# A selective-scan phase in which two gate blocks take their Silu after the scan, by an exponential and a reciprocal, and VectorE makes the first input product

## The reference, cut to what matters

```python
x_and_res = x @ in_proj_w.T + in_proj_b
x_b, res = jnp.split(x_and_res, [D_INNER], axis=-1)
...
x_b = jax.nn.silu(jnp.transpose(xc, (0, 2, 1)))
...
delta = jax.nn.softplus(delta @ dt_proj_w.T + dt_proj_b)
a = -jnp.exp(A_log)
y = _selective_scan(x_b, delta, a, b, c)   # h = exp(delta a) h + delta b x_b ; y = h c
y = y + x_b * D_param
y = y * jax.nn.silu(res)
return y @ out_proj_w.T + out_proj_b
```

## Time and profile before

| | us |
|---|---|
| median of 3 runs | 728.68 (724.33 to 729.57) |
| profiled execution | 728.93 |
| its span, first to last instruction | 727.2 |
| mean granted clock of TensorE, share of full | 0.962 |
| busy: PE, DVE, ACT, POOL | 667.5, 471.7, 367.1, 223.1 |

### The profile page before, as it was taken

How to read it: one execution, slowest core, us unless ns; L and a number is a source line. 1 busy time by engine, 2 the same in 40 slices (tenths; PEclk the granted TensorE clock), 3 DMA queues, 4 the chain that set the end, 5 groups by cost and what they waited for, 6 DMA issues and landing times. The chain is left out here.

```text
span 727.2 us, 11254 instructions
## 1 busy us (share of the span) xinstructions
PE 667.5 (92%) x4226; PEld 466.1 (64%) x4226; DVE 471.7 (65%) x809; ACT 367.1 (50%) x677; POOL 223.1 (31%) x181
## 2 busy tenths in 40 slices
PE   3989999999994999998989999899899989999998
PEld 1445555553353656565556788787777667889897
DVE  5123433448737998999989337576777658676554
ACT  1222111215476998998988333432456337447442
POOL 2000000000008999998976000032543002222000
PEclk9999999999996999999999999999989879999999
DMA  8999999738121232222220000000100012110000
GB/s 317 371 379 401 420 421 420 314 114 258 35 87 59 87 116 88 104 100 88 107 82 16 1 1 15 1 0 17 32 2 3 1 59 73 45 58 2 29 1 30
DMA packets 31069, 86.45 MB, mean 119 GB/s; under 512 B 7900, under 2 KB 19576, under 8 KB 28840
## 3 DMA queue, kind: packets, MB, share of 16 engines
q1 hardware_dynamic: 30456, 85.28, 32.2%
q10 hardware_dynamic: 560, 0.46, 0.3%
HBM read 83.50 MB, written 1.11 MB: 116 GB/s over the span
## 5 line engine op out<-in xcount | busy, mean ns | idle before, releaser
L683 POOL TENSOR_TENSOR dbu<-du,bs 128x1024 f32<-128x1024 f32 x64 | 150.8, 2375 | 227.6 <-DVE du L890 214.9
L1003 PE MATMUL Y<-weighed,ident 128*128 128x512 f32 (+1 forms) x256 | 101.8, 519 | 0.0
L900 DVE TENSOR_TENSOR_SCAN w_in<-A,dbu 128x1024 f32<-128x1024 f32 x42 | 95.1, 2275 | 0.0
L776 ACT ACTIVATE weighed<-T,CT 128x256 f32<-128x256 f32 x208 | 83.1, 477 | 18.2 <-PE T L993 16.7
L765 ACT ACTIVATE A<-delta,negA 128x504 f32<-128x504 f32 x128 | 83.4, 697 | 3.7 <-DVE xn L900 3.7
L1003 PEld LDWEIGHTS Y<-weighed,ident 128*128 128x128 f32 x256 | 44.0, 193 | 29.8 <-issue 29.2
L993 PE MATMUL T<-ident,w_in 128*128 128x128 f32 x336 | 45.9, 281 | 7.9 <-ACT weighed L776 2.7
L993 PEld LDWEIGHTS T<-ident,w_in 128*128 128x128 f32 x336 | 38.0, 144 | 23.4 <-DVE w_in L900 12.5
L900 DVE TENSOR_TENSOR_SCAN xn<-A,dbu 128x1024 f32<-128x1024 f32 x22 | 50.1, 2276 | 2.9 <-POOL dbu L683 2.3
L253 PE MATMUL S<-cT,qkT 128*64 128x512 f32 (+1 forms) x256 | 46.5, 517 | 0.8 <-issue 0.8
L265 PE MATMUL O<-cN,pT 128*64 128x256 f32 x384 | 46.7, 385 | 0.0
(11 more groups left out here) (409 smaller groups left out, 1365.3 us busy)
## 6 DMA issues: line engine op xcount, KB each, us to landing
cT<-in_ctxT SPq DMA_DIRECT2D x8, 3202.0 KB, 14.8
cN<-in_ctx SPq DMA_DIRECT2D x8, 3072.0 KB, 13.9
bs<-b_rows SPq DMA_DIRECT2D x32, 512.0 KB, 3.6
raw_w<-in_w SPq DMA_DIRECT2D x16, 256.0 KB, 2.9
w<-in_w SPq DMA_DIRECT2D x7, 256.0 KB, 8.0
vs<-vx SPq DMA_DIRECT2D x8, 136.0 KB, 2.4
x<-in_x SPq DMA_DIRECT2D x2, 512.0 KB, 5.8
cR<-in_ctx SPq DMA_DIRECT2D x1, 1024.0 KB, 31.8
```

Source lines behind the costliest of these rows:

```text
L683: e.tensor_tensor(dbu[s % NB][:, :, :], half(m.du, s // DS), row, ALU.mult).then_inc(s_bu, 1)
L776: i = e.activation(weighed[s % 2][:, q * Q:(q + 1) * Q], T[:, q * Q:(q + 1) * Q], ACT.Copy, scale=c_of(s, q))
L900: e.tensor_tensor_scan(S[s % NS], A[s % 2][:, :], dbu[s % NB][:, :, :].rearrange("p c n -> p (c n)"), 0.0, ALU.mult, ALU.add).then_inc(s_h, 1)
L1003: e.matmul(Y[:, w], k.ident[:, :], weighed[s % 2][:, w], start=False, stop=True, skip_group_check=True).then_inc(s_y, 1)
```

## The change

Seven things are done together:
- `gate_part(6)` and `gate_part(7)` leave ACT's program. In their place DVE adds the bias and writes the raw blocks to `m.sres` (`raw_gate`), and the PE's transposes that reuse `T` wait for these (`s_rg`) in place of ACT's last gate;
- ACT no longer waits for DVE's `positive` steps ahead of the exponentials;
- behind the loop over the scan's steps ACT makes exp(-x) and adds one, for the two late blocks, into unused parts of `m.delta` (`late`); DVE takes the reciprocal and multiplies it into `m.sres` (four instructions), ahead of `close` of the last unit; the last unit's `gate` waits for these;
- the addition of the output bias to `k.x` is cut into two halves (`output_bias`), one ahead of and one behind the copies of step `("vo", 0)`;
- DVE makes the input product of step 0, `dbu[0]`, and POOL starts with step 1;
- the copies of step `("vo", 1)` stand behind that product, so that `add_parts(0)`, `add_parts(1)` and `du` come ahead of them;
- `add_parts(2)` and `add_parts(3)` move from before the scan to behind scan(1) and scan(2).

The diff, without its first piece, which only declares the five new semaphores:

```diff
@@ -602,7 +607,7 @@
         ac_steps = [("xb", 1), ("u", 0), ("xb", 2), ("xb", 3), ("u", 1), ("xb", 4), ("u", 2), ("xb", 5), ("xb", 6), ("u", 3),
                     ("xb", 7), ("u", 4), ("u", 5), ("gate", 0), ("gate", 1), ("u", 6), ("abs", 0), ("abs", 1), ("gate", 2),
                     ("abs", 2), ("abs", 3), ("u", 7), ("gate", 3), ("gate", 4), ("abs", 4), ("abs", 5), ("gate", 5),
-                    ("abs", 6), ("abs", 7), ("gate", 6), ("gate", 7), ("exp", 1), ("exp", 0), ("ln", 0), ("ln", 1), ("ln", 2),
+                    ("abs", 6), ("abs", 7), ("exp", 1), ("exp", 0), ("ln", 0), ("ln", 1), ("ln", 2),
                     ("neg", 0), ("CT", 0), ("wT", 0), ("wT", 1)]
         pe_at = {step: i + 1 for i, step in enumerate(pe_steps)}
         ac_at = {step: i + 1 for i, step in enumerate(ac_steps)}
@@ -610,6 +615,8 @@
 
         def out(t, n):
             return A[t // 4][:, (t % 4) * D:(t % 4 + n) * D]
+
+        late = [m.delta[:, 2 + c, 0:HALF] for c in range(2)]
 
         def landed(s):
             return m.s_bs[(s // 2) % SLOTS], 16 * (s // 2 // SLOTS + 1)
@@ -642,8 +649,9 @@
             e.wait_ge(k.s_w2, k.n_w2 + 16)
             for g in range(SLOTS):
                 load_states(e, m, g)
+            e.wait_ge(s_b0, 1)
             for g in range(SLOTS, STEPS // 2):
-                e.wait_ge(s_bu, 2 * (g - SLOTS) + 2)
+                e.wait_ge(s_bu, 2 * (g - SLOTS) + 1)
                 load_states(e, m, g)
 
         @block.gpsimd
@@ -662,19 +670,17 @@
                 hs = slice(h * HALF, (h + 1) * HALF)
                 e.tensor_tensor(m.du[:, c, hs], m.delta[:, c, hs], m.u[:, c, hs], ALU.mult).then_inc(s_dup, 1)
 
-            for s in range(STEPS):
+            for s in range(1, STEPS):
                 if s in (3, 6):
                     steps_by_input(0, s // 3 + 1)
                 if s in (9, 12, 21, 24):
                     add_parts((9, 12, 21, 24).index(s))
                 if s in (15, 18, 34, 37):
                     steps_by_input(1, (15, 18, 34, 37).index(s))
+                if s == 1:
+                    e.wait_ge(s_du, 2)
                 if s % DS == 0:
-                    u = s // DS
-                    if u == 0:
-                        e.wait_ge(s_du, 2)
-                    else:
-                        e.wait_ge(s_dup, (2, 6, 10)[u - 1])
+                    e.wait_ge(s_dup, (2, 6, 10)[s // DS - 1])
                 sem_, n = landed(s)
                 e.wait_ge(sem_, n)
                 if s >= NB:
@@ -739,9 +745,6 @@
             gate_part(5)
             absolute(6)
             absolute(7)
-            gate_part(6)
-            gate_part(7)
-            e.wait_ge(s_rz, 2 * CH)
             e.wait_ge(s_fa, ac_at["abs", 7])
             a0, aw = COLS["alog"]
             e.activation(expA[:, :], k.cols[:, a0:a0 + aw], ACT.Exp).then_inc(s_fa, 1)
@@ -803,6 +806,13 @@
                     weigh(s, b)
                     if first:
                         keep_sum(u, 1 - b)
+            e.wait_ge(s_rg, 2)
+            e.wait_ge(s_A, 2 * DS)
+            for c in range(2):
+                e.activation(late[c], m.sres[:, 2 + c, HALF:2 * HALF], ACT.Exp, scale=-1.0).then_inc(s_gx, 1)
+            for c in range(2):
+                e.wait_ge(s_gx, c + 1)
+                e.activation(late[c], late[c], ACT.Identity, bias=1.0).then_inc(s_ge, 1)
             for b in range(2):
                 keep_sum(len(UNITS) - 1, b)
             for w in range(2):
@@ -869,8 +879,20 @@
             for n in range(CH, 2 * CH):
                 positive(n)
             e.wait_ge(k.s_rows, 16)
-            e.tensor_tensor(k.x[:, :, :], k.x[:, :, :],
-                            rowvec(k, "outb").unsqueeze(1).to_broadcast([P, TILES, D]), ALU.add)
+
+            def raw_gate(n):
+
+                e.wait_ge(s_fp, pe_at["in", 8 + n])
+                e.tensor_scalar(m.sres[:, n % CH, HALF:2 * HALF], zp[n % 4], col(k, "inb", CH + n % CH), None, ALU.add
+                                ).then_inc(s_rg, 1)
+
+            def output_bias(g):
+                ts = slice(HT * g, HT * (g + 1))
+                e.tensor_tensor(k.x[:, ts, :], k.x[:, ts, :], rowvec(k, "outb").unsqueeze(1).to_broadcast([P, HT, D]), ALU.add)
+
+            raw_gate(6)
+            raw_gate(7)
+            output_bias(0)
             e.wait_ge(s_fa, ac_at["abs", 7])
             e.wait_ge(s_rz, 2 * CH)
             e.wait_ge(s_xe, 2)
@@ -880,21 +902,27 @@
             e.wait_ge(s_fa, ac_at["u", 2 * CH - 1])
             e.tensor_copy(bvT, spare[:, 0:KD])
             e.tensor_copy(vT, T[:, HALF:2 * HALF]).then_inc(s_vo, 1)
-            e.wait_ge(s_fp, pe_at["vo", 1])
-            e.tensor_copy(k.wfq[0:1, :], spare[0:1, 0:D])
-            e.tensor_copy(k.w5v[:, :, 0:D], T[:, HALF:2 * HALF].rearrange("p (c n) -> p c n", c=KD)).then_inc(s_vo, 1)
+            output_bias(1)
             for c in range(2):
                 add_parts(c)
             for c in range(2):
                 e.wait_ge(s_dl, c + 1)
                 e.tensor_tensor(m.du[:, c, 0:HALF], m.delta[:, c, 0:HALF], m.u[:, c, 0:HALF], ALU.mult).then_inc(s_du, 1)
-            for c in range(2, CH):
-                add_parts(c)
+            e.wait_ge(s_du, 2)
+            e.wait_ge(landed(0)[0], landed(0)[1])
+            e.tensor_tensor(dbu[0][:, :, :], half(m.du, 0), m.bs[0][:, 0, :].unsqueeze(1).to_broadcast([P, 2, HALF]), ALU.mult
+                            ).then_inc(s_b0, 1)
+            e.wait_ge(s_fp, pe_at["vo", 1])
+            e.tensor_copy(k.wfq[0:1, :], spare[0:1, 0:D])
+            e.tensor_copy(k.w5v[:, :, 0:D], T[:, HALF:2 * HALF].rearrange("p (c n) -> p c n", c=KD)).then_inc(s_vo, 1)
             e.wait_ge(s_z, 2)
 
             def scan(s):
                 e.wait_ge(s_A, s + 1)
-                e.wait_ge(s_bu, s + 1)
+                if s:
+                    e.wait_ge(s_bu, s)
+                else:
+                    e.wait_ge(s_b0, 1)
                 if s >= NS:
                     e.wait_ge(s_t, 2 * (s - NS) + 2)
                 e.tensor_tensor_scan(S[s % NS], A[s % 2][:, :], dbu[s % NB][:, :, :].rearrange("p c n -> p (c n)"),
@@ -924,6 +952,8 @@
 
             def gate(u, j):
                 e.wait_ge(s_tt, 2 * u + j + 1)
+                if u == len(UNITS) - 1:
+                    e.wait_ge(s_gd, 4)
                 b = j if u == len(UNITS) - 1 else 0
                 g = half(m.sres, u)[:, j, :]
                 h, cp = UNITS[u]
@@ -934,12 +964,20 @@
             for s in range(STEPS):
                 if s + 1 < STEPS:
                     scan(s + 1)
+                if s < 2:
+                    add_parts(2 + s)
                 if on_dve(s):
                     weigh(s)
                 if s and s % DS == 0:
                     close(s // DS - 1)
                 if turned(s):
                     gate(*turned(s))
+            for c in range(2):
+                g = m.sres[:, 2 + c, HALF:2 * HALF]
+                e.wait_ge(s_ge, c + 1)
+                e.reciprocal(late[c], late[c]).then_inc(s_gd, 1)
+                e.wait_ge(s_gd, 2 * c + 1)
+                e.tensor_tensor(g, g, late[c], ALU.mult).then_inc(s_gd, 1)
             close(len(UNITS) - 1)
 
             def residual(g):
@@ -1062,7 +1100,8 @@
             dt_proj(7)
             project(14)
             project(15)
-            e.wait_ge(s_fa, ac_at["gate", 2 * CH - 1])
+            e.wait_ge(s_fa, ac_at["gate", 5])
+            e.wait_ge(s_rg, 2)
             e.wait_ge(s_xe, 2)
             e.wait_ge(s_dg, 1)
             for t in range(TILES):
```

More of the change, by code:

```diff
@@ L578, in mamba @@
         s_dg = sem("m_dg")
+        s_rg = sem("m_rg")
+        s_gx = sem("m_gx")
+        s_ge = sem("m_ge")
+        s_gd = sem("m_gd")
+        s_b0 = sem("m_b0")
         s_z = sem("n_z")
```

## The result

The changed kernel takes 732.08 us in the median of 12 runs (727.63 to 732.69), the kernel before 728.71 (724.28 to 730.28). The ratio is 1.0041, with a 95% interval from 1.0022 to 1.0059: slower by 0.4%, within 1%. The profiled execution took 732.69 us and has a span of 731.0, against 727.2 before.

The account below looks back on a forecast made before the run. POOL was taken to set the pace up to step 15, DVE behind it. From 728.93 us, the head's 4.4 came off, the tail's 5.0 and the clock's 2.0 were added: 731.5 us, range 725.5 to 736.0.

Parts of the forecast that it names:

- a slow reciprocal with a falling clock: Main case at the tail: R near 2.9 us and PE's clock falling, 730 to 733.5 us, forecast 731.5, chance 0.55.
- Head: Ahead of the scan: scan(0) 5.7 us earlier, scan(15) 4.4 us earlier, bounds 3.9 and 5.0, carried to scan(63).
- POOL's unbroken run: From 220.94 to about 265.1 in the kernel before, POOL works without a break; its end sets scan(15) at 265.23.
- That is nil: Ahead of the scan: PE's transposes waiting for raw block 7 on DVE cost nothing; `("vo", 1)` still ready at 217.4.
- `add_parts(3)`: In the scan's first steps: the moved sum of 0.64 us on DVE takes about 0.6 us from POOL's run.
- 2R - 0.77: Behind the scan: us by which the tail is later, with two reciprocals ahead of `close`; 5.0 us forecast.
- R: Time of one 128x512 reciprocal on DVE, 2.9 us, from a slope of 5.4 ns an element in narrow rows.
- Clock: PE's 4.9 us idle ahead of the turn brings half speed for 3.5 to 6.6 us behind it; 2.0 us taken.
- the fast reciprocal: Rival at the tail: R = 0.69 us like any 512-wide operation, tail 0.6 us later, 725.1 us; chance 0.12.
- eight passes: Rival at the tail: 8 ns an element, R 4.2 us, tail 7.7 us later, middle 735 us; chance 0.10.
- the smaller head: Rival: copies of `("vo", 1)` hold scan(0), head gains some 2.5 us, 733.4 us; chance 0.08.
- The change does nothing at the head: Rival ahead of the scan: ACT's table load still waits for something; no more than a part of the 0.08 case.

Follow-up runs that it names:

- e_silu_sum2_first: Changed kernel with the late blocks by ACT's Silu behind the scan and `add_parts(2)` on DVE ahead of `du`; 721.68 us, 0.9903 of the kernel before.
- e_add2_early: Changed kernel with `add_parts(2)` on DVE ahead of the copies of the folded weights, not behind scan(1); 731.29 us, 1.0038 of the kernel before.
- e_sums_first: Changed kernel with `add_parts(2)` and `add_parts(3)` right behind `du`, ahead of step 0's product; 731.79 us, 1.0039 of the kernel before.
- e_pe_kept_busy: Changed kernel with 36 unread transposes in PE's idle ahead of the last sum's turn; 729.96 us, 1.0021 of the kernel before.
- e_act_only: Kernel before with only gates 6 and 7 off ACT and the late Silu by ACT behind the scan; 728.99 us, 0.9997 of the kernel before.

## Why the prediction was right

The forecast was 731.5 us and the measurement 732.08; the case was the likeliest, a slow reciprocal with a falling clock. By its steps:

- **Head.** ACT's load at 205.76 (205.6), scan(0) at 218.77 (218.7), POOL's idle of 2.41 us (2.4), `du` at 223.91 (223.8), scan(15) at 260.78 (260.8), the last scan at 394.34 (394.4). The reading that POOL's unbroken run sets scan(15), and that the row's own releaser was not it, held. e_silu_sum2_first moves the start of POOL's unbroken run (its `du` is 17.02 us behind ACT's last `absolute` and not 18.86), and scan(15) follows by 1.9 us.
- **"That is nil"** for the raw blocks on DVE: PE's step ended within 0.2 us of before.
- **`add_parts(3)`** was priced at 0.6 us of POOL. POOL lost 0.45 (7.45 for three products against 7.00). That DVE would lose 1.03 us too was not seen; it cost nothing that shows here, since POOL was busy without a break from 223.9 to 260.8, and it is what failed e_add2_early and e_sums_first.
- **The tail's formula** 2R - 0.77 was right and R too small: 3.35 us and not 2.9. It gives 5.9 with the measured R; measured are 5.60 from the last scan to the turn. What is over in R is 0.45 us an instruction; the formula was 0.3 too high elsewhere, since ACT's pairs of activations were quicker and the first reciprocal started 6.36 us behind the last scan's start and not 6.69. The straight line through the narrow reciprocals gave 5.4 ns an element, the wide one shows (3349 - 178) / 508 = 6.2. An element of a reciprocal costs six ordinary ones here, between the line and the eight. The Trainium skill (VectorE: DVE Perf Modes, "First, the fixed hardware budget") states a repeat count of 8 and no time; eight ordinary elements for one, as the rival read it, is not what these rows show.
- **Clock.** 2.0 us taken, 1.76 measured, and e_pe_kept_busy shows that idle is its cause. The 3.5 us at the low end of its range stood there without a row; the stretch behind the turn was that long.
- **Not in the sum**: 0.87 us behind the barrier, from where the clock falls in unchanged code. The prediction looked at the clock up to the barrier only. It had no term for the 1.7 us that the kernel before lost right behind it and the changed one didn't, nor for the longer half clock near 530; that these came to as little as 0.87 is luck.
- **The total.** The sum's parts that belong to the change make -4.54 + 5.60 + 1.76 = 2.8 us, where 2.6 were forecast. The closeness owes something to luck: the tail was 0.6 us too small, the clock 0.24 too large and the head's gain 0.14 too small. That the median came out at 3.4 and not at 2.8 is luck of the same size as these misses.
- **The rivals** fall: the fast reciprocal and eight passes by R, the smaller head by scan(0).
- **"The change does nothing at the head"** was given no chance of its own. e_act_only shows how near it was: without the other order on DVE, ACT's 3.6 us are worth nothing.

## What to carry to other kernels

Work that is moved out of a stage costs by what is queued behind it in its new place: two reciprocals cost 5.6 us in front of `close` with their input late, and 0.2 us around it with their input early; and the same Silu on an engine that was waiting there cost nothing. Where two engines end a stage together, moving one of them shows nothing until the other moves too, so an edit should be tested in both halves. And two-input products from SBUF on VectorE are best put where GpSimd is not in such an instruction: ahead of `du` a sum took 0.63 us, beside POOL 1.70 to 2.84.

## What the runs showed that I had not expected

- VectorE and GpSimd hold each other for whole instructions, either way. A 128x512 sum of 0.67 us took 1.70, 2.78 and 2.84 us when it was issued while POOL was in a product of 2.35 us, and three DVE instructions of 2.5 us took 6.7. POOL's first product, where its median is 2.36, took 3.33 us beside two DVE sums and 3.38 beside a DVE product. The Trainium skill (SBUF — State Buffer, "SBUF: two separate sides") states this: the port pair that the two share is an exclusive lock, held for the full instruction, also by a VectorE operation with two SBUF inputs. The traces agree, and the prediction had read the earlier trace rows as a cost to POOL alone.
- A 128x512 reciprocal on VectorE takes 3.35 us, five times a product of that size.
- After 5.4 us of idle on PE the run behind it was at half clock for 3.5 us (granted clock 0.50 from 409.8 to 413.3): 1.94 us for eight transposes instead of 1.04. In one long unchanged stretch the length went with the clock's falls, from 171.1 to 174.0 us from kernel to kernel, as much as most of these edits; what an edit does is better read between rows near it.
- Half clock behind the barrier, 3.4 us long, came in eight of the nine executions without the long idle ahead of the turn, and the full clock there in three of the five with it. Whether it, and the longer one near 530, follow from the shift of the work ahead of them or are chance stays open: no run varied the shift alone.
